# Two operand layouts of a float32r matmul kernel: parts kept in buffers of their own, and parts woven into one buffer

## The reference

```
x = x + L0(x)      # x: 128 rows x 64 heads x 1024
x = x + L1(x)
L0: x @ base_weight.T + base_bias + (x @ A[id].T) @ B[id].T   # a rank-16 adapter chosen by row
L1: a long convolution of each head over the 1024 places (an S4D filter K of 64 modes, through an FFT),
    plus u * D, masked by each row's length
```

## Time and profile before

| what | value |
|---|---|
| median of 3 runs | 1070.8 us (1069.19 to 1071.14) |
| the profiled execution | 1069.73 us |
| its span, first to last instruction | 1068.0 us |
| granted TensorE clock over the span | 1.000 of full speed |

### The profile page before, as it was taken

The page is one execution under the profiler, slowest core; times in us unless marked ns, Lnnn a source line. Parts: engine busy times, 40 slices in busy tenths (PEclk is TensorE's granted clock), DMA queues, the critical chain, the costliest instruction groups (busy, mean ns, idle before and its releaser), DMA issues.

```text
span 1068.0 us, 21568 instructions
## 1 busy us (share of the span) xinstructions
PE 1061.2 (99%) x8088; PEld 1028.8 (96%) x8088; DVE 848.5 (79%) x1263; ACT 717.0 (67%) x1260; POOL 28.6 (3%) x79
## 2 busy tenths in 40 slices
PE   9999999999999999999999999999999999999998
PEld 7999999999999999999999999999989999999997
DVE  7899887878698787878778787877488888888886
ACT  5755545755747466556557467465598888888885
POOL 0000000000000000000000000000010000000000
PEclk9999999999999999999999999999999999999999
DMA  8586758688786978868785888858798978798873
GB/s 290 202 304 221 275 191 284 199 300 307 226 269 211 298 225 277 282 229 275 229 308 179 296 260 259 293 194 283 264 346 286 350 287 335 294 326 317 304 263 123
DMA packets 162586, 284.62 MB, mean 266 GB/s; under 512 B 10739, under 2 KB 125620, under 8 KB 149044
## 3 DMA queue, kind: packets, MB, share of 16 engines
q1 hardware_dynamic: 162484, 283.26, 77.1%
HBM read 193.96 MB, written 89.26 MB: 265 GB/s over the span
## 4 chain that ended last, share of the span: by engine, by line
PE 97%; DVE 1%; ACT 1%; DMA 0%; issue 0%; DVEq 0%; SPq 0%; ACTq 0%
PE acc L1810 37%; PE acc L1970 25%; PE acc L1816 18%; PE acc L1738 5%; PE acc L1782 5%; PE acc L2005 3%; PE acc L1748 2%; DMA x_raw<-x_t 0%; PE acc L1915 0%; ACT x_hi L687 0%; PE acc L1774 0%; DVE x_sb L1262 0%; ACT L845 0%; ACT L851 0%; DVE g_sb L1460 0%
## 5 line engine op out<-in xcount | busy, mean ns | idle before, releaser
L1970 PE MATMUL acc<-u_hi,f_hi 128*128 128x512 f32 (+1 forms) x320 | 128.9, 403 | 0.0
L687 ACT ACTIVATE acc<-acc 128x512 f32<-128x512 f32 x93 | 54.0, 581 | 109.4 <-PE acc L1816 109.3
L1810 PE MATMUL acc<-t_hi,v_lo 128*128 128x256 f32 x512 | 123.0, 279 | 0.0
L1810 PE MATMUL acc<-t_hi,v_hi 128*128 128x256 f32 x512 | 122.9, 279 | 0.0
L1810 PE MATMUL acc<-t_hi,w_pair 128*128 128x256 f32 x960 | 122.4, 279 | 0.0
L1970 PE MATMUL acc<-u_lo,f_hi 128*128 128x512 f32 (+1 forms) x320 | 118.4, 370 | 0.0
L1970 PE MATMUL acc<-u_hi,f_lo 128*128 128x512 f32 (+1 forms) x320 | 118.2, 369 | 0.0
L1810 PEld LDWEIGHTS acc<-t_hi,w_pair 128*128 128x128 f32 x960 | 116.9, 188 | 0.0
L687 ACT ACTIVATE t_hi<-t_raw 128x1024 fp32r<-128x1024 f32 x64 | 67.9, 1061 | 61.7 <-DVE t_raw L1220 33.0
L1105 DVE TENSOR_TENSOR t_lo<-t_raw,t_hi 128x1024 fp32r<-128x1024 f32 x64 | 78.3, 1223 | 34.3 <-ACT t_hi L687 33.9
L1810 PEld LDWEIGHTS acc<-t_hi,v_lo 128*128 128x128 f32 x512 | 96.2, 188 | 0.0
(11 more groups left out here) (205 smaller groups left out, 2673.3 us busy)
## 6 DMA issues: line engine op xcount, KB each, us to landing
w_pair<-weight_scratch SPq DMA_DIRECT2D x71, 1024.0 KB, 6.5
x_scratch<-x_sb SPq DMA_DIRECT2D x32, 1024.0 KB, 6.0
out<-out_sb SPq DMA_DIRECT2D x63, 512.0 KB, 4.8
x_raw<-x_t SPq DMA_DIRECT2D x15, 2048.0 KB, 11.1
u_raw<-x_scratch SPq DMA_DIRECT2D x14, 2048.0 KB, 11.8
wq_raw<-state_scratch SPq DMA_DIRECT2D x16, 1024.0 KB, 8.1
a_raw<-lora_a SPq DMA_DIRECT2D x128, 64.0 KB, 5.7
b_raw<-lora_b SPq DMA_DIRECT2D x128, 64.0 KB, 2.1
```

Of the source, the lines that this page charges most:

```text
L687: return act.activation(dst, src, ACT.Copy)
L1810: pe.matmul(by_row(bank_part(bank, i)), w[:, k, i, :], hi[:, k, :, :], start=opens and i == 0 and k == 0 and s == 0, stop=False, skip_grou ...
L1970: mm = pe.matmul(bank, w, m, start=first and i == 0, stop=last and i == 2, skip_group_check=onto_closed)
```

## The change

The high and the low part of x go into one buffer `x_parts`, `[P, 8 tiles, 64 heads, 2 parts, 8 rows]`: half c of one part is then a run of 4 words in every 16, and a whole row of one part a run of 8 in every 16. The two high and three low slots of the sums go into one buffer `t_parts`, `[P, 4, 64 heads, 5 slots, 4]`, with the high parts in slots 0 and 1 and the sums and low parts in slots 2 to 4: runs of 4 words in every 20. All that writes or reads these tiles follows: ScalarE's and VectorE's splits, the sums, adapters_down, the plain products. The number and size of instructions stays. `zeros` moves to where `zb` lies, and the wait for its transfer moves from ScalarE's first T2 split to VectorE, ahead of `even_sums`, which is the first to write there. `u_raw` lies over the second and the first half of `x_parts`.

```diff
-    x_hi_at = cursor[0]
-    x_hi = place("x_hi", [P, NT, N], F32R)
-    x_lo_at = cursor[0]
-    x_lo = place("x_lo", [P, NT, N], F32R)
+    XHI, XLO = range(2)
+    x_at = cursor[0]
+    x_parts = place("x_parts", [P, NT, heads, 2, G], F32R)
+    X_HALF = HALF * heads * 2 * G * 4
...
-    t_lo = place("t_lo", [P, HALF, heads, 3, GH], F32R)
-    t_raw = place("t_raw", [P, HALF, heads, 3, GH], F32, at=t_at)
-    t_hi_at = cursor[0]
-    t_hi = place("t_hi", [P, HALF, heads, 2, GH], F32R)
-    t4_raw = place("t4_raw", [P, NT, N], F32, at=x_lo_at)
+    T_SLOTS = 5
+    t_parts = place("t_parts", [P, HALF, heads, T_SLOTS, GH], F32R)
+    t_raw = place("t_raw", [P, HALF, heads, T_SLOTS, GH], F32, at=t_at)
+    t4_raw = place("t4_raw", [P, NT, heads, 2, G], F32, at=x_at)
...
-    zeros = place("zeros", [heads, KPAD], F32, at=t_hi_at)
+    zeros = place("zeros", [heads, KPAD], F32, at=zb_at)
...
-    LO_SLOT = {"T1": 2, "T2": 0, "T3": 1, "T4": 0}
+    LO_SLOT = {"T1": 4, "T2": 2, "T3": 3, "T4": 2}
...
-    u_raw = [place(f"u_raw{i}", u_shape, F32, at=at) for i, at in enumerate((x_raw_at, x_hi_at, x_lo_at))]
+    u_raw = [place(f"u_raw{i}", u_shape, F32, at=at) for i, at in enumerate((x_raw_at, x_at + X_HALF, x_at))]
...
+    def x_row(part, t):
+        return x_parts[:, t, :, part, :]
...
+    def x_part(part, r, c):
+        return x_parts[:, r * HALF:(r + 1) * HALF, :, part, c * GH:(c + 1) * GH]
...
+    def x_half(part, t, c):
+        return x_parts[:, t, :, part, c * GH:(c + 1) * GH]
...
-        return block(t4_raw, 0, 1) if n == "T4" else t_raw[:, :, :, LO_SLOT[n], :]
+        return t4_raw[:, 0:HALF, :, XLO, GH:G] if n == "T4" else t_raw[:, :, :, LO_SLOT[n], :]
...
-                copy(x_hi[:, t, :], x_raw[:, t, :]).then_inc(c_xhi, 1)
+                copy(x_row(XHI, t), by_column(x_raw[:, t, :])).then_inc(c_xhi, 1)
...
-                if g == 0 and n == "T2":
-                    act.wait_ge(st_pad, 16)
-                copy(t_hi[:, :, :, HI_SLOT[n], :], t_source(g, n)).then_inc(c_thi[n], 1)
+                copy(t_parts[:, :, :, HI_SLOT[n], :], t_source(g, n)).then_inc(c_thi[n], 1)
...
                 dve.wait_ge(ld_e, 16 * 4)
+                dve.wait_ge(st_pad, 16)
...
-                minus_hi(x_lo[:, t, :], x_raw[:, t, :], x_hi[:, t, :]).then_inc(c_xlo, 1)
+                minus_hi(x_row(XLO, t), by_column(x_raw[:, t, :]), x_row(XHI, t)).then_inc(c_xlo, 1)
...
-                product_hi(bank, w_hi, w_lo, block(x_hi, r, c), opens)
-                return product_lo(bank, w_hi, block(x_lo, r, c))
+                product_hi(bank, w_hi, w_lo, x_part(XHI, r, c), opens)
+                return product_lo(bank, w_hi, x_part(XLO, r, c))
...
-                product_hi(bank, w_hi, w_lo, t_hi[:, :, :, HI_SLOT[n], :], opens)
+                product_hi(bank, w_hi, w_lo, t_parts[:, :, :, HI_SLOT[n], :], opens)
...
-                return product_lo(bank, w_hi, t_lo[:, :, :, LO_SLOT[n], :])
+                return product_lo(bank, w_hi, t_parts[:, :, :, LO_SLOT[n], :])
```

More of the change, by code:

```diff
@@ L302, in block, with by_column @@
         return t[:, r * HALF:(r + 1) * HALF, :].rearrange("p k (h a b) -> p k h a b", a=2, b=GH)[:, :, :, c, :]
+    def x_row(part, t):
[4 more added lines that the diff above has]
+        return x_parts[:, t, :, part, c * GH:(c + 1) * GH]
+    def by_column(ap):
+        return ap.rearrange("p (h b) -> p h b", b=G)
     def half(t, c):
@@ L1229, in split_t @@
                 dve.wait_ge(c_thi[n], g + 1)
-                minus_hi(t_lo[:, :, :, LO_SLOT[n], :], t_source(g, n),
-                         t_hi[:, :, :, HI_SLOT[n], :]).then_inc(c_tlo[n], 1)
+                minus_hi(t_parts[:, :, :, LO_SLOT[n], :], t_source(g, n),
+                         t_parts[:, :, :, HI_SLOT[n], :]).then_inc(c_tlo[n], 1)
             def split_a(g):
@@ L1736, in adapters_down @@
                         pe.wait_ge(c_xlo, NT * g + t + 1)
-                        for i, m in enumerate((x_hi, x_lo)):
+                        for i, part in enumerate((XHI, XLO)):
                             mm = pe.matmul(half(acc[:, H_BANK, :], c),
                                            a_st[:, t, c, :, :].rearrange("p k r -> p (k r)"),
-                                           half(m[:, t, :], c), start=t == 0 and i == 0, stop=t == NT - 1 and i == 1)
+                                           x_half(part, t, c), start=t == 0 and i == 0, stop=t == NT - 1 and i == 1)
                     mm.then_inc(m_h, 1)
@@ L1745, in plain_products @@
                 c, kk = divmod(k, HALF)
-                pairs = products([w_pair[:, 2 * r + c, s, kk, ii, :] for s in range(2)], (x_hi[:, k, :], x_lo[:, k, :]))
+                pairs = products([w_pair[:, 2 * r + c, s, kk, ii, :] for s in range(2)], (x_row(XHI, k), x_row(XLO, k)))
                 for s, (w, m) in enumerate(pairs):
-                    mm = pe.matmul(acc[:, plain_bank(i), :], w, m, start=k == 0 and s == 0, stop=False)
+                    mm = pe.matmul(by_column(acc[:, plain_bank(i), :]), w, m, start=k == 0 and s == 0, stop=False)
                 return mm
```

## The result

The changed kernel takes 1126.85 us (median of 4, 1126.52 to 1127.26) against 1070.69: ratio 1.0527, interval 1.0509 to 1.0545. It is 56.2 us slower, where 7 us less was forecast; the range, to 1077, doesn't reach it.

A forecast was written before the change was run, and what follows sets the result against it. TensorE, never short of work, was taken to bound the kernel by matmul count times distance between starts. Gains of 4.1 us (x) and 3.0 us (sums' high parts), 7.1 in all, gave 1063.5 us, range 1054 to 1077.

The forecast's parts named there:

- I take 115.8 ns, the nearest wider spacing that was measured: TensorE's 2744 matmuls on x, from every 8 to every 16 words: 1.5 ns less each, gain 4.1 us.
- same argument, same value: High parts of the sums, from every 8 to every 20 words: 1984 matmuls at 1.5 ns less, gain 3.0 us.
- 0 for the low ones: Low parts of the sums, from every 12 to every 20 words: already at 115.8 ns, so no gain; bounds +9 and -7 us.
- The estimate for adjacent columns: A matmul of 256 adjacent columns, not in the trace: 122.7 ns, from 176 less 128 columns at 2.4 GHz.
- The observation under it: Matmuls on the sums' low parts, 4 words in every 12, take 1.5 ns less than the others; ascribed to layout or place.
- the gap doesn't matter: Rival: the 1.5 ns comes from place or other engines; x and high parts stay at 117.3 ns; 1069 to 1072 us, chance 0.20.
- The rule that the prediction had set against its own sum: SBUF reads: a run of 4 words fills its 16-byte line before as after, so the gain is 0 instead of 7.1 us.
- x dearer: Rival: 64-byte hops make TensorE's reads wait in the 2744 matmuls on x; 1073 to 1083 us, chance 0.25.
- The sums' bound that the prediction kept from adjacent columns: Matmuls on sums cost at most 122.7 ns, the dearest layout estimated: loss at most 11 us for high parts, 7 for low.

The follow-up runs named there:

- The probes: Kernel before plus 24 matmuls for each candidate layout, results overwritten; whole time says nothing; runs of 4 words every 20 took 133.3 ns a matmul.
- the last kernel: Kernel before with the same 52 KB laid out so that nearly every operand is 4 words in every 12: 1063.15 us against 1069.99, ratio 0.9933.
- the 64-partition probes: Probes in the kernel before, reading only the first 64 partitions, every 12 to 24 words: 133.3 ns at a hop of 20, 160 ns at 24.
- the first probe run: Kernel before plus 24 matmuls for each of 36 layouts read out of v_hi, in three groups: 24 in 3.20 us for 4 words in every 20.
- the run with fewer partitions: Kernel before plus probes of 24 matmuls, runs of 4 words, on 128, 64 and 32 partitions: 133.3 ns with 64 partitions at a hop of 20.
- the second probe run: Kernel before plus 24 matmuls for each of 58 more layouts, hops by steps of 4 words: 512 columns, 4 in every 20, took 266.7 ns.

## Why the prediction was wrong

The bound was read rightly: TensorE's distance between starts sets the time, and next to nothing else moved: no wait was added, the splits kept their durations, the second stage took 300.4 us against 300.3, and the plain products lost 0.12 us in 24.

The step that failed is the price of the two new hops, "I take 115.8 ns, the nearest wider spacing that was measured", with "same argument, same value" for the high parts of the sums and 0 for the low ones. It took three points, one of them an estimate, for a curve in the size of the gap. The probes show no such curve: 119.5, 117.9, 114.6, 121.6, 133.3, 160, 121, 127.5 ns for hops of 4 to 32 words, and hops of 68 to 112 words cost what 4 to 48 do. The estimate for adjacent columns, 122.7, was 3 ns too high, which made the fall look steeper. In place of the sums' gain of 3.0 us came 1984 x 15.9 + 992 x 18.0 = 49.4 us; 49.1 were measured with the sums alone. In place of x's 4.1 us of gain came 4.9 of loss by itself, and some 2 to 3 more in company.

The observation under it held: the 1.5 ns by which the old low parts were cheaper belonged to the hop of 12 words, as the last kernel shows, where the high parts have that hop and reach 113 to 116 ns. One reading of it was off: the 1.5 ns doesn't show "in all 8 pieces of this group". One of T1's two is as long as x's:

```profile
526.25 0.94 PE acc L1816 x8
```

T1's low part lay in the third of the three slots, and with a hop of 12 words the probe from there takes 2.80 us for 24, 116.7 ns, against 114.6 from the first.

So "the gap doesn't matter" was wrong too. The rule that the prediction had set against its own sum fared no better. The Trainium skill, Advanced Engine Details and Errata, Memory Cachelines, says that accesses to the same 16-byte line run at full performance and that at least two on a line are needed. The runs agree with the 16 bytes as a unit and not with the rest: full lines cost up to 43 ns more than the 117.3 of before, by the hop, and with two words of each line 256 columns take 230 ns where they take 119.5 with four.

The rival that ended on the other side, x dearer, came nearest: it looked for a price that depends on the address, and had the wrong hop. It feared 64 bytes, which cost x 1.2 to 4.1 ns, and not 80, which cost 16 to 18. That a divided memory is behind the price fits the period of 256 bytes, but no run shows it. The sums' bound that the prediction kept from adjacent columns, 11 + 7 us, was no bound: nothing in the trace said that adjacent columns are the dearest layout.

What stays open: why hops of 80, 96, 208 and 256 bytes are the dear ones and 112 isn't. That the price isn't one that partitions make for each other rests on the 64-partition probes alone. Also open is what moves runs in every 16 words between 114 and 126 ns, and why the first word of a layout matters.

## What to carry to other kernels

When TensorE reads an operand in short runs, the hop from run to run has a price of its own, which isn't monotone in its size and repeated with 256 bytes here; two measured hops don't give a third. Before a layout is changed, put 24 matmuls for each candidate hop into the kernel as a probe and read their pieces in the chain: one run sorted 58 layouts here, and a kernel built on the cheapest hop took 0.7% less. Read the granted clock of each probe with its piece. Weaving by itself was the smaller part of the cost: the same five parts woven with another order of dimensions took 40 us less.

## What the runs showed of the hardware that was not expected

Runs of 8 words can be dear as well: 8 in every 40 take 133 ns, 8 in every 32 115.

The time of two dear layouts did not follow TensorE's clock: 2 words in every 24 took 320 ns a matmul at 2.4 GHz and at 1.2 GHz (L1817 above), 2 words in every 32 took 246 ns at 2.4 GHz and 247 at 1.2.

TensorE's granted clock fell to half in three places although TensorE was busy throughout. Two stretches of the first probe run, then one of the run with fewer partitions (us, then busy time and count for TensorE, its weight loads, VectorE, ScalarE and GpSimd, then granted clock, DMA share, GB/s):

```profile
641.00:642.60 1.60, 1.60 (x6) 1.11 (x5) 0.00 (x0) 0.00 (x0) 0.00 (x0) 1.00 0.00 0
...
645.00:648.40 3.40, 3.40 (x13) 3.40 (x12) 0.00 (x0) 0.00 (x0) 0.00 (x0) 0.50 0.00 0
```

```profile
475.00:510.00 35.00, 35.00 (x166) 35.00 (x166) 0.00 (x0) 2.74 (x4) 0.00 (x0) 0.50 0.18 56
```

The first two lie in the probe with 2 words in every 24, with all 128 partitions and after 28 us of other 2-word probes at 1.00; the third is matmuls of 32 partitions at 1.2 GHz. The third place is the last 64-partition probe: from 370.60 to 374.00 us the granted clock was 0.75 in the mean, and its piece took 4.55 us where 128 partitions took 3.84. The 58 layouts of the second probe run, all with 128 partitions and runs of 4 words or more, ran at 1.00. So TensorE back to back without a gap was not enough here to hold the clock up, and few partitions were not needed for the fall.
